# Two 16-head attentions of 64 with one more buffer of exponentials and another order of work; a third attention with other queue orders and its scores interleaved over two pairs of heads

## The reference, cut to what matters

```
L0, L3:  16 heads of 64           L2:  16 heads of 16, keys masked
q, k, v = split(h @ Wqkv)         # h: normalised and modulated x
(L3 alone: q = LN(q)*g + b, k = LN(k)*g + b over the 64 of a head)
attn = softmax(q @ k.T * d**-0.5) # d = 64 or 16
x = x + gate * ((attn @ v) @ Wout)
```

## Time and profile before

| | us |
|---|---|
| median of 3 runs | 3348.43 (3346.29 to 3350.02) |
| the profiled execution | 3351.11 |
| its span | 3349.3 |
| TensorE busy | 3035.8 (91%) |
| weight loads | 2517.6 (75%) |
| VectorE busy | 2157.1 (64%) |
| ScalarE busy | 1695.7 (51%) |
| GpSimd busy | 893.6 (27%) |

### The profile page before, as it was taken

How to read it: one execution, slowest core, us unless ns; L and a number is a source line. 1 busy time by engine, 2 the same in 40 slices (tenths; PEclk the granted TensorE clock), 3 DMA queues, 4 the chain that set the end, 5 groups by cost and what they waited for, 6 DMA issues and landing times. The chain is left out here.

```text
span 3349.3 us, 70763 instructions
## 1 busy us (share of the span) xinstructions
PE 3035.8 (91%) x26089; PEld 2517.6 (75%) x26090; DVE 2157.1 (64%) x4193; ACT 1695.7 (51%) x3085; POOL 893.6 (27%) x725
## 2 busy tenths in 40 slices
PE   7999999997998989999999699799999999993797
PEld 5887888776998978877777598577777777772686
DVE  4555665655666766577777467666666666667674
ACT  3444444443553445455444455566666666661464
POOL 2333223232112321122222211313131313130453
PEclk8999999998999999999999799899999999996898
DMA  5000000001001000000000100100000000003353
GB/s 170 4 6 6 6 3 6 6 6 35 19 21 44 0 23 0 22 7 8 8 9 9 46 19 19 35 1 0 0 0 0 0 0 0 0 13 117 86 141 64
DMA packets 68976, 80.66 MB, mean 24 GB/s; under 512 B 10146, under 2 KB 61090, under 8 KB 68884
## 3 DMA queue, kind: packets, MB, share of 16 engines
q1 hardware_dynamic: 62756, 71.14, 7.2%
q0 software_dynamic: 6144, 8.52, 1.3%
HBM read 66.80 MB, written 12.85 MB: 24 GB/s over the span
## 5 line engine op out<-in xcount | busy, mean ns | idle before, releaser
L956 POOL TENSOR_TENSOR L3a_shift<-L3a_neg,L3a_mx 128x256 fp32r<-128x256 f32 x128 | 94.8, 740 | 523.1 <-DVE L3a_mx L1556 523.1
L1063 ACT ACTIVATE L0a_prob<-L0a_st 128x512 f32<-128x512 f32 x256 | 134.1, 602 | 162.1 <-PE L0a_st L1293 74.3
L945 POOL TENSOR_TENSOR L0a_o<-L0a_prob 128x1024 f32<-128x1024 f32 x48 | 118.8, 2476 | 303.7 <-PE L0a_o L1330 303.7
L1063 ACT ACTIVATE L3a_prob<-L3a_st 128x512 f32<-128x512 f32 x256 | 133.8, 602 | 117.7 <-POOL L3a_o L945 90.0
L1925 ACT ACTIVATE L2a_prob<-L2a_st 128x512 f32<-128x512 f32 x256 | 132.2, 604 | 117.9 <-PE L2a_st L1958 117.9
L1556 DVE TENSOR_REDUCE L0a_mx<-L0a_s 128x2 f32<-128x512 f32 x224 | 143.7, 683 | 74.7 <-PE L0a_s L1267 74.7
L1546 DVE SCALAR_TENSOR_TENSOR L3a_qk_lo<-raw,cols_sb,L3a_qk_hi 128x256 fp32r<-128x256 f32 x256 | 158.1, 657 | 36.5 <-ACT L3a_qk_hi L1054 36.5
L1556 DVE TENSOR_REDUCE L3a_mx<-L3a_s 128x2 f32<-128x512 f32 x256 | 163.7, 679 | 15.6 <-PE L3a_s L1267 15.6
L2190 DVE TENSOR_REDUCE L2a_mx<-L2a_s 128x2 fp32r<-128x512 f32 x256 | 163.5, 681 | 15.3 <-PE L2a_s L1958 15.3
L1157 PE MATMUL L0a_st<-L0a_xt,home 128*128 128x256 f32 x512 | 150.3, 294 | 5.1 <-DVE home L1664 5.1
L1158 PE MATMUL L0a_st<-L0a_xt,home 128*128 128x256 f32 x512 | 145.7, 285 | 0.0
(11 more groups left out here) (615 smaller groups left out, 11232.5 us busy)
## 6 DMA issues: line engine op xcount, KB each, us to landing
raw<-in_moe_w SPq DMA_DIRECT2D x16, 1024.0 KB, 8.6
x_sb<-in_x SPq DMA_DIRECT2D x1, 4096.0 KB, 24.7
L0a_gate<-gate_rows SPq DMA_DIRECT2D x32, 128.0 KB, 3.9
L0m_gate<-gate_rows SPq DMA_DIRECT2D x32, 128.0 KB, 3.8
L2a_gates<-gate_rows SPq DMA_DIRECT2D x32, 128.0 KB, 3.8
L2m_gate<-gate_rows SPq DMA_DIRECT2D x32, 128.0 KB, 3.8
out_x<-x_sb SPq DMA_DIRECT2D x1, 4096.0 KB, 16.9
token_rows<-x_sb SPq DMA_DIRECT2D x1, 4096.0 KB, 29.0
```

Of the source, the lines that this page charges most:

```text
L945: nc.gpsimd.tensor_tensor(half_sums, both[:, :, :, 0:N], both[:, :, :, N:2 * N], ALU.add).then_inc(halves_done, 1)
L956: nc.gpsimd.tensor_tensor(shift[:, u % 4, :, :, :], neg64[:].unsqueeze(1).unsqueeze(1).to_broadcast([P, 2, TT, 64]), mx[:, u % 2, :, :].un ...
L1063: A(prob[:, u % 4, h, :], st_ps[u % 2][h][:], ACT.Exp, scale=64 ** -0.5).then_inc(p_done, 1)
```

## The change

In `heads64`:

- Except in the last step, pair 1 has a buffer of its own (`spare`: the idle weight stage in L0a, a part of `raw` in L3a), pair 2 the second half of `prob` and pair 3 the first. The exponentials of pair 1 no longer wait for `x_low`, those of pair 2 do, and nothing waits for `halves`.
- VectorE: `x_low(i+1)` moves from between maxes(4) and maxes(5) to behind maxes(5) (in L3a behind qn_low(5)), in L0a right ahead of `add`. In L0a `take` moves ahead of maxes(2). In L3a qn_low(2) moves ahead of maxes(2), with `take` behind it; o_low(0) moves ahead of the next sample's `modulate`.
- L3a: TensorE runs qk(3) ahead of over(0); ScalarE runs qn_high(0) behind raw_copy(7) and not behind raw_copy(6).

In `heads16`:

- The exact scores of both pairs are one loop, pair by pair inside each product, except at u = 1 of all steps but the last.
- TensorE runs over(0) and over(1) of u = 1 behind `qk` and `max_rows`. VectorE: both over's behind shift and qk_low, both o_low's in u = 2, x_low between the two reductions of one maxes. ScalarE: o_high(0) behind qk_high.

```diff
+            w_stage = sb("w_stage", [P, 2, 1024])
+            spare = w_stage[:].rearrange("p u (h n) -> p u h n", h=2)
+        else:
+            spare = raw[:, 0:PAIRS, :].rearrange("p (u h) n -> p u h n", h=2)
+        pair_prob = lambda p, last: prob[:, 2 * p % 4:2 * p % 4 + 2, :, :] if last else (prob[:, 0:2, :, :], spare, prob[:, 2:4, :, :], prob[:, 0:2, :, :])[p]
+        head_prob = lambda u, h, last: pair_prob(u // 2, last)[:, u % 2, h, :]
...
-                        if c >= 6:
-                            qn_high(c - 6)
+                        if c == 7:
+                            qn_high(0)
+                            qn_high(1)
...
-                    if p == 1 and not final:
+                    if p == 2 and not final:
                         act.wait_ge(xlo_done, i + 2)
-                    if p in (2, 3):
+                    if p in (2, 3) and final:
                         act.wait_ge(halves_done, 3 * i + p - 1)
...
                     qk(2)
+                    qk(3)
                     last_over(0)
-                    qk(3)
                     last_over(1)
...
                     last_over(1)
+                    last_o_low(0)
                     if not final:
                         modulate(i + 1)
-                    last_o_low(0)
...
                 for p in range(PAIRS):
+                    if p == 0 and gated and not first:
+                        take(i - 1)
+                    if p == 0 and qknorm:
+                        qn_low(2)
                     if p + 1 < PAIRS:
                         maxes(2 * p + 2)
-                    if p == 1 and not final:
-                        x_low(i + 1)
-                    if p == 0 and not first:
+                    if p == 0 and qknorm and not first:
                         take(i - 1)
-                    if qknorm and p < 3:
+                    if qknorm and p in (1, 2):
                         qn_low(2 * p + 2)
                     if p + 1 < PAIRS:
                         maxes(2 * p + 3)
                     if qknorm and p < 3:
                         qn_low(2 * p + 3)
+                    if p == 1 and not final:
+                        x_low(i + 1)
                     if p == 1 and gated and not first:
                         add(i - 1)
```

heads16, TensorE:

```diff
-            def body(i, first, final):
-                def scores_t(w):
+                def scores_t(u, pairs):
...
-                            for h in range(2):
-                                last = mm(st_ps[w % 2][h][:, kt * N:(kt + 1) * N], a[rows(w, h), w // 2, ks], b[rows(w, h), w // 2, 0:N],
+                            for w in pairs:
+                                for h in range(2):
+                                    last = mm(st_ps[w][h][:, kt * N:(kt + 1) * N], a[rows(w, h), u, ks], b[rows(w, h), u, 0:N],
...
-                    if u == 1 and not first:
-                        pe.wait_ge(p_done, 4 * slot + 3)
-                        over(i - 1, 0)
-                        over(i - 1, 1)
...
                         max_rows(u + 1)
+                    if u == 1 and not first:
+                        pe.wait_ge(p_done, 4 * slot + 3)
+                        over(i - 1, 0)
+                        over(i - 1, 1)
```

More of the change, by code:

```diff
@@ L939, in output_weights, with halves @@
                     nc.gpsimd.tensor_tensor(wo[1][:, cs, :], src, wo[0][:, cs, :].bitcast(F32), ALU.subtract).then_inc(wo_done, 1)
-            def halves(i, p):
+            def halves(i, p, last):
                 gated_wait(pv_done, PAIRS * i + p + 1)
-                both = prob[:, 2 * p % 4:2 * p % 4 + 2, :, :]
+                both = pair_prob(p, last)
                 nc.gpsimd.tensor_tensor(half_sums, both[:, :, :, 0:N], both[:, :, :, N:2 * N], ALU.add).then_inc(halves_done, 1)
@@ L957, in shift_of, with body @@
                                             mx[:, u % 2, :, :].unsqueeze(3).to_broadcast([P, 2, TT, 64]), ALU.mult).then_inc(shift_done, 1)
-                def body(i):
+                def body(i, last=False):
                     for u in range(6):
                         shift_of(i, u)
-                    halves(i, 0)
+                    halves(i, 0, last)
                     shift_of(i, 6)
                     shift_of(i, 7)
-                    halves(i, 1)
-                    halves(i, 2)
+                    halves(i, 1, last)
+                    halves(i, 2, last)
                 token_rstd(1)
@@ L974, in _ @@
                     body(i)
-                body(B - 1)
+                body(B - 1, last=True)
             else:
@@ L979, in o_low, with body @@
                     nc.gpsimd.tensor_tensor(o_lo[:, n % 2, :], o32[:, n % 2, :], o_hi[:, n % 2, :].bitcast(F32), ALU.subtract).then_inc(olo_done, 1)
-                def body(i, first=False):
+                def body(i, first=False, last=False):
                     if not first:
@@ L985, in body @@
                     for p in range(3):
-                        halves(i, p)
+                        halves(i, p, last)
                     tail(i)
@@ L1930, in body @@
                             row_high(i - 1)
-                    if u == 1 and not first:
-                        o_high(i - 1, 0)
                     if u == 0 or not final:
@@ L1937, in body @@
                     if u == 1 and not first:
+                        o_high(i - 1, 0)
                         o_high(i - 1, 1)
@@ L2063, in body @@
                         pe.wait_ge(on_done, PIECES * i)
-                    scores_t(2 * u)
                     if u == 1 and not final:
+                        scores_t(u, (0,))
                         pe.wait_ge(xlo_done, i + 2)
-                    if u == 3 and not first:
-                        pe.wait_ge(taken, i)
-                    scores_t(2 * u + 1)
+                        scores_t(u, (1,))
+                    else:
+                        if u == 3 and not first:
+                            pe.wait_ge(taken, i)
+                        scores_t(u, (0, 1))
                     if u == 0 and not first:
@@ L2183, in qk_low, with maxes @@
                 V.tensor_tensor(qk_lo[:, c, :], ring[bank][:], qk_hi[:, c, :].bitcast(F32), ALU.subtract).then_inc(qklo_done, 1)
-            def maxes(pair, w):
-                for h in range(2):
+            def maxes(pair, w, heads=(0, 1)):
+                for h in heads:
                     dve.wait_ge(s_done, 2 * pair + h + 1)
@@ L2201, in body @@
                     ahead = not final or u < U - 1
-                    if ahead:
+                    if ahead and u == 1 and not final:
+                        maxes(2 * slot + 2, 2 * u + 2, (0,))
+                        x_low(i + 1)
+                        maxes(2 * slot + 2, 2 * u + 2, (1,))
+                    elif ahead:
                         maxes(2 * slot + 2, 2 * u + 2)
@@ L2206, in body @@
                     if u == 2 and not first:
-                        o_low(i - 1, 1)
+                        o_low(i - 1, 0)
                     if u == 3 and not first:
@@ L2213, in body @@
                         row_low(i - 1)
+                    if u == 2 and not first:
+                        o_low(i - 1, 1)
+                    if ahead:
+                        shift(slot + 1, (u + 1) % U)
+                    if u == 0 or not final:
+                        qk_low(U * i + u + 3, (u + 3) % U, 0)
                     if u == 1 and not first:
@@ L2216, in body @@
                         over(i - 1, 1)
[L2217 to L2224, removed]
                     if u == 2 and not first:
```

15 lines of the change are left out of this document (7 added, 8 removed).

## The result

The changed kernel takes 3404.98 us (median of 4 runs, 3402.09 to 3407.03), the kernel before in the same comparison 3348.39 us (4 runs). The ratio is 1.0169, with an interval of 1.0154 to 1.0185: slower by 56.6 us. Forecast were 3370 us with a range of 3340 to 3386. The direction was right, the size was not, and the time lies outside the range.

The account below looks back on a forecast made before the run. TensorE, busy 94 to 98% at a granted clock of 0.99 to 1.00, was taken to set the end. L0a +22, L2a -14 and L3a +14 made +22 us on 3348.4: 3370 us, range 3340 to 3386.

Parts of the forecast that it names:

- The block at halves(0): L0a's add and L3a's x_low stand until GpSimd's halves(0) ends: net +22 us in L0a, +14 us in L3a.
- the port costs nothing: Rival for L0a and L3a: x_low and add run beside halves without loss; total 3317 us, chance 12%.
- add or x_low escapes: Two rivals: L0a's add precedes halves (3349 us, 14%), or L3a's x_low precedes halves(0) (3345 us, 7%).
- qn_high(0): L3a: ScalarE's later qn_high(0) delays qn_low(0) by 1.2 us, set off at 0 against gains of 0.65 and some 0.4.
- the block at halves(0) swallows most of either: L3a: the stand behind halves(0) hides most of the offset's ends, -0.6 and +1.2 us a step.
- L2a: Reordering and interleaved scores take 1.0 us less a step, about 14 us less; ends 0 and 22 us.
- The interleaving: L2a's exact scores of two pairs interleaved: 0.1 us a step; a rival had 0.35 at every unit, 3360 us, 4%.
- the gathering of four: L2a: interleaved exact scores make 6 rounds of 4 matmuls out of 9 mixed rounds, 0.35 us less.
- take and the buffers: L0a's take ahead of maxes(2): 0.38 us a step less, 5.7 us; buffers in L0a and L3a: nothing by themselves.

Follow-up runs that it names:

- e4: e1 plus four reductions of one SBUF tile on VectorE in each middle step of L0a and L3a, results unused: 3401.7 us.
- e7: e1 plus two reductions of one SBUF tile on VectorE in each middle step of L0a and L3a, results unused: 3337.03 us.
- e1: The changed kernel with x_low alone put back between maxes(4) and maxes(5) in L0a and L3a: 3319.96 us, ratio to the kernel before 0.9912.
- e6: e1 with ScalarE's qn_high(0) of L3a also back behind raw_copy(6): 3303.65 us, ratio to the kernel before 0.9859.
- e9: The changed kernel with ScalarE's qn_high(0) of L3a alone back behind raw_copy(6): 3396.28 us.
- e10: The kernel before with only the new buffers and x_low moved behind maxes(5), in L3a behind qn_low(5): 3440.59 us.

## Why the prediction was right in direction and wrong in size

- **The block at halves(0): right.** Its place, its cause and its length are in both attentions as forecast. The steps without half clock are 1.77 us (L0a) and 0.84 us (L3a) longer; forecast were 1.6 and 0.9. The rivals by which the port costs nothing, or add or x_low escapes, are out: add was blocked in 14 of 15 steps (in the last it goes first, as in the kernel before), x_low of L3a in all 15. A lead of 0.12 us was enough. The list of VectorE's operations with both inputs in SBUF, ahead of the prediction, is one short: L0a's `shift` is one too, and it stood behind halves(0) in each middle step of the kernel before, 1.30 us against 0.43:

```profile
410.25 1.30 DVE L1559 TENSOR_TENSOR L0a_shift<-L0a_neg,L0a_mx 128x256 fp32r<-128x256 f32 x1
```

- **The clock: the step of the sum that failed.** "TensorE is busy 98% ... all at a granted clock of 0.99 to 1.00" was read as a constant and then every microsecond of waiting was priced at one microsecond. No term of the sum is for the clock. In those steps TensorE never stood longer than 0.6 us; the change makes it stand 2.2 and 2.7, and e4 and e7 show that the falls come with waits of this length. "The timelines repeat from step to step within 0.05 us" was a misreading too: in L2a two of the 14 steps take 30.29 us and not 28.76, with 3.4 us at half clock in each. The mean step is longer than the shortest by 1.13 us in L0a (15.8 us over 14) and 1.32 in L3a (18.5 us): 34.3 of the 34.6 us between 56.6 and 22. That these agree so closely is in part chance, since the points below are off by some us to either side and cancel.
- **qn_high(0): its size was right, its swallowing wrong.** Its loss was taken as 1.2 us a step and set off at 0 against gains of about 1.05 around it. e1 and e6 give 1.11 for it. Moving x_low costs L3a 1.23 at full clock (56.70 against 55.47; the forecast's 1.7 less the 0.65 at x_low's old place is 1.05), and all else is worth -1.50 (e6 against before; the forecast had 0.8 and 0.4). 1.23 + 1.11 - 1.50 is the 0.84 measured. But the claim that "the block at halves(0) swallows most of either" was wrong: e9 has the gain beside the block. The block was priced as if all ahead of it could be late for nothing; but halves(0) and x_low move with what is ahead of them.
- **L2a: right, a little low.** Forecast -1.0 us a step, measured -1.24 from step to step of the usual kind (28.76 to 27.52) and -1.48 in the mean: the two steps of 30.29 us are gone. That part is luck: e10, whose L2a is that of the kernel before, has no such step either. The interleaving is about the 0.1 taken; the gathering of four is real and hidden behind the first exponential.
- **take and the buffers: right, take a little high.** 0.27 us a step in e1 (47.24 to 46.97) against 0.38; buffers 0. The move of x_low costs L0a 2.04 us at full clock (49.01 against 46.97), forecast 2.0.
- **The ends.** L2a's last step is 2.3 us longer than before (34.59 against 32.30); TensorE idles 9.9 us in it against 7.3 and is at half clock for 19.1 against 16.0, and which edit does it stays open. L0a's last step is 2.0 us longer (52.22 against 50.20, forecast 0.4 shorter), and that is the clock: the wait of 2.83 us ahead of scores(7) stands in both kernels, and in e1, where no fall comes with it, the step takes 49.75 us. TensorE before, then after:

```profile
790.83 0.50 PE L1267 MATMUL L0a_s<-L0a_qk_hi 64*128 64x256 f32 x4 [2.83 <-DVE L0a_mx L1556]
...
791.38 0.64 PE L1345 MATMUL L0a_sum<-L0a_o,L0a_sum_sel 128*32 128x256 f32 x8
```

```profile
826.98 0.80 PE L1274 MATMUL L0a_s<-L0a_qk_hi 64*128 64x256 f32 x4 [2.83 <-DVE L0a_mx L1563]
...
827.92 1.08 PE L1352 MATMUL L0a_sum<-L0a_o,L0a_sum_sel 128*32 128x256 f32 x8
```

The trace before allowed a better range. The two new waits are over 4 times the longest that TensorE had in the middle steps, so their steady clock was no evidence for them; the one wait of such a length there (2.83 us, above) had no fall behind it, but it was one case. And the 0.99 of L2a in the earlier trace rows said that a busy engine can lose its clock. A term of 0 to 1.7 us a step for the clock (half of 3.4 us, the length of L2a's falls) belonged in the range, if not in the sum. That is 0 to 24 us for each attention, and takes the range to 3410 with one of them and to 3434 with both.

## What to carry to other kernels

Before an operation with two inputs in SBUF is moved on VectorE, look at what GpSimd does at the new time, and by how much it comes first: 0.1 to 0.25 us decided over some 2.2 us here. Price a wait of the engine that sets the end twice, once for its length and once for the clock at which it comes back; a new wait that is much longer than any in the old trace leaves the range in which the old clock is evidence. And where a change of many parts is slower, take it apart before it is dropped: one line of this one cost 85 us, another 16, and without these two it beats the kernel before by 47 us (ratio 0.9859).

## What the runs showed of the hardware that was not expected

The clock of a TensorE that is busy 92 to 95% of the time fell to 1.2 GHz with waits of 2.0 to 2.8 us, for 3.4 or 6.8 us, and in part of the steps only: with the same wait of 2.23 us 10 of 14 steps in L0a had a fall, and with the same 2.66 us 9 of 14 steps in L3a. Waits of up to 0.9 us (L0a) and 1.1 us (L3a) in e7 had none. A fall of 3.4 us costs 1.2 to 1.7 us and one of 6.8 us 2.5 or 2.6: 16 matmuls in it take 3.57 us and not 1.95. In L3a of the changed kernel the steps from the third on repeat in threes (no fall, 3.4 us, 6.8 us), and the wait of 2.83 us in L0a's last step, the same in all twelve kernels, comes with 0, 3.4 or 6.8 us at half clock in 2, 4 and 6 of them.

Long waits are not the only occasion: the kernel before has two falls in L2a, in steps whose longest wait is 0.5 us. TensorE, kernel before, in such a step and in the next one:

```profile
1652.29 0.39 PE L1958 MATMUL L2a_st<-L2a_rsum_hi,L2a_spread 128*128 128x256 f32 x1 [0.46 <-ACT L2a_prob L1925]
...
1653.69 1.48 PE L1958 MATMUL L2a_st<-L2a_xt,L2a_wq 128*128 128x256 f32 x6
...
1683.64 0.87 PE L1958 MATMUL L2a_st<-L2a_xt,L2a_wq 128*128 128x256 f32 x6
```

Two of 14 steps had it there, and none of 14 in e10, with the same L2a code and the same waits. The Trainium skill ("TensorE: Matmul & The Clock Gate", section "Part 1: The HAM clock gate") has the two levels, and that the engine's recent activity picks between them. The traces agree with the first (0.50 and 1.00 are all they show); with the second they agree where a long wait comes ahead, and the two falls in L2a they don't explain. Which of equal waits comes with a fall, no run here was made to tell.
